# Moving weight-only work of a cross-attention into the feed-forward block in front of it, on one Trainium2 core

## The chip, the cores and the metric

One core of a Trainium2 chip runs the whole program. The metric is the device time of one execution in microseconds (us), as the median of several runs. The engines are named as in the profile: PE (TensorE, matmuls), PEld (its weight loads), DVE (VectorE), ACT (ScalarE), POOL (GpSimd), SP (SyncE, which here only issues DMAs).

## The reference, cut to what matters

Six blocks follow each other on a stream x of 512 rows by 512 columns; each adds its result to x and each starts with a layer norm over the columns. The change touches blocks 3, 4 and 5.

```python
def _layernorm(x, axis=-1, eps=1e-05):
    m = jnp.mean(x, axis=axis, keepdims=True)
    v = jnp.var(x, axis=axis, keepdims=True)
    return (x - m) / jnp.sqrt(v + eps)
...
    x = x + _L0_ffn_ref(_layernorm(x, axis=-1), ...)                 # block 3: w1, depthwise conv, silu, w2, both products quantised
    x = x + _L1_xattn_ref(ctx_1024, _layernorm(x, axis=-1), ...)     # block 4
    x = x + _L1_attn_ref(_layernorm(x, axis=-1), ...)                # block 5
...
    def _L1_xattn_ref(x, latents, Wq, Wkv, Wout, gm, bm, gl, bl):    # x is the context of 8192 rows
        xn = layernorm(x, gm, bm)
        ln = layernorm(latents, gl, bl)                              # a second norm of an already normed tensor
        q = ln @ Wq
        kv_input = jnp.concatenate([xn, ln], axis=-2)
        kv = kv_input @ Wkv
...
        xn = _l2norm(x) * dim ** 0.5 * gamma                         # block 5: unit rows of an already normed tensor
```

## The kernel before

Each engine has one program, written in order by hand; the engines meet through counting semaphores. A float32 product is done as three passes over two parts of each operand (`product`, three matmuls: low by high, high by low, high by high), so each operand is first split into a rounded high part (usually by ACT) and a remainder (by DVE or POOL). The context is handled in 17 chunks of 512 keys; chunk 0 are the latents (the 512 rows of x), chunks 1 to 16 are the context. `cT_raw`, `cT_hi`, `cT_lo` hold a chunk and its halves, two slots in turn.

The work around the change, in the order of PE:

- Block 3. The rows of the normed x are quantised on DVE and ACT (`xq_s`, `xq`), transposed on PE, and a row of factors is spread over the partitions by a matmul with diagonal matrices (`diagonals` on DVE, `spread` on PE, `scale_all` on ACT). Then 16 blocks hb of 128 hidden features: PE multiplies (4 matmuls into one of two banks), DVE scales (`pre_conv`), ACT and DVE do the convolution of three taps, ACT the silu and the absolute value, DVE the running maximum (`col_max`, by `largest`). PE may be two blocks ahead of DVE. Then the maximum is transposed, made into factors, spread again by `diagonals(…, 1)` and `spread(1)`, the hidden rows are scaled and rounded in eight pieces (`hidden_s`, `hidden_q`), and PE does the second product, whose four row blocks come out one after another.
- Block 4, preparation. DVE adds each row block to x and norms it twice (`TWICE`: the order of the two norms of four row blocks). POOL computes the two reciprocal roots of each. PE transposes the rows. `sd` (a reciprocal of the context's scales) is split and transposed. PE multiplies `wkv_raw` by `b_ctx` in matmuls of one column (`bv`). DVE subtracts to get `wq_lo`; it applies gain and offset (`affine_rows`) and splits (`xT_hi`, `xT_lo`). PE computes the queries, then the keys of chunk 0 with `wkv_hi`, `wkv_lo`. For the context the weights are used in another form, `wp_hi`, `wp_lo`: `wkv_raw` times the gain `g_ctx`, minus its column mean (a PE sum with `ones`). Their order on PE is queries, keys, column sum, values. ACT copies chunk 1 into `cT_hi`, POOL subtracts for `cT_lo` after it has set `peak` to its starting value, and only then `project_pe(1, …)` starts: the long loop over the chunks, in which PE also computes similarities of the chunk before for the row maximum.
- Block 5. As in block 4 each row block is added and normed, then squared and summed on ACT, and made a unit row by POOL (power) and DVE (`unit_row`).

The DMAs of all this are issued by SP in a fixed order: the quantised weights (`w_q`) while block 2 ends; `wq_raw`, `wkv_raw` and two context chunks after the last output of block 3's second product.

## Time and profile before

| | |
|---|---|
| time, median of 3 runs | 2752.25 us (2751.64 to 2753.24) |
| the profiled execution: its own time / its span | 2750.85 / 2749.1 us |
| PE, PEld, DVE busy | 2521.2 (92%), 1681.8 (61%), 1842.6 us (67%) |
| ACT, POOL busy | 1106.4 (40%), 566.0 us (21%) |
| block 3 and the preparation of block 4 | about 799 to 963 us of the span |
| the norm of block 5 | about 1981 to 1993 us |

The busy share of an engine is an average over blocks with different limits. The change lies in two stretches, which have to be read by themselves: which engine works there, which waits, and what ends its wait. The time of the profiled execution is 1.75 us above its span, and 1.4 us below the median of the runs.

### The profile page before, as it was taken

The page shows a single profiled execution, that of the slowest core. Times are in us where ns is not written, and L with a number is a line of the kernel's source. Part 1 is how long each engine was busy: PE and PEld are TensorE (multiplying, and loading weights), DVE is VectorE, ACT ScalarE, POOL GpSimd, SP SyncE. Part 2 cuts the span into 40 slices and gives each one's busy share as a digit, 9 for nine tenths or more (in the row PEclk, how much of TensorE's full clock was granted, in tenths as well). Part 3 has the DMA queues.
Part 4 walks back from the last instruction along what each step waited for, and adds up shares of the span by engine and source line. Part 5 has one row for each costly group of instructions (what it writes and reads, how often), then busy time and mean ns, then how long its engine had stood idle before and what let it go on. Part 6 is the DMA issues. An engine that isn't in the chain of part 4 may idle for free.

```text
span 2749.1 us, 33961 instructions
## 1 busy us (share of the span) xinstructions
PE 2521.2 (92%) x11615; PEld 1681.8 (61%) x11618; DVE 1842.6 (67%) x2026; ACT 1106.4 (40%) x1344; POOL 566.0 (21%) x413
## 2 busy tenths in 40 slices
PE   6999988967765799999999999999898799999999
PEld 5778867722222677777765454555477677777775
DVE  5878753189988677778886666666535666666665
ACT  2334422244435322222235555555332455555453
POOL 4555552078850211111110000000100100000000
PEclk9999989999986899999999999999889899999999
DMA  7677745710010233433423332333200366666663
GB/s 281 235 238 261 262 119 161 275 52 16 15 69 12 103 135 135 160 145 132 159 97 109 110 97 66 96 111 96 81 31 31 153 230 224 222 224 219 218 227 134
DMA packets 123659, 394.68 MB, mean 144 GB/s; under 512 B 23664, under 2 KB 39228, under 8 KB 97072
## 3 DMA queue, kind: packets, MB, share of 16 engines
q1 hardware_dynamic: 95584, 326.82, 33.5%
q10 hardware_dynamic: 27984, 66.66, 7.0%
q8 instruction: 56, 0.92, 0.1%
q14 instruction: 35, 0.29, 0.0%
HBM read 304.14 MB, written 89.30 MB: 143 GB/s over the span
## 4 chain that ended last, share of the span: by engine, by line
PE 78%; DVE 10%; DMA 5%; issue 3%; POOL 2%; ACT 1%; ACTq 0%; DVEq 0%; SPq 0%; POOLq 0%
PE ps L2130 18%; PE ps L2131 16%; PE ps L2132 16%; PE ps L2481 10%; PE ps L2491 9%; DVE ps L1632 4%; PE ps L2389 3%; DMA w_halves<-unit_lo 3%; PE ps L2742 1%; DMA wT_lo<-w_halves 1%; DVE drive L1632 1%; PE ps L2283 1%; POOL drive L907 1%; DMA sh_raw<-in_s_parts 1%; DVE ln_st L1478 1%
## 5 line engine op out<-in xcount | busy, mean ns | idle before, releaser
L1877 DVE TENSOR_TENSOR sums<-sums,pT 128x1024 f32<-128x1024 f32 x272 | 319.2, 1221 | 194.0 <-ACT pT L1302 192.9
L1815 DVE SCALAR_TENSOR_TENSOR peak<-ps,rs_all,peak 128x1024 f32<-128x1024 f32 x272 | 335.6, 1278 | 95.0 <-PE ps L2389 94.6
L1302 ACT ACTIVATE pT<-ps,rs_all 128x1024 f32<-128x1024 f32 x272 | 284.9, 1112 | 230.7 <-PE ps L2481 230.4
L2491 PE MATMUL ps<-pT,values 128*64 128x512 f32 x1088 | 256.4, 602 | 0.0
L2235 PE MATMUL ps<-read,ident 128*128 128x512 f32 x256 | 143.7, 673 | 73.8 <-DVE read L1638 37.2
L907 POOL TENSOR_TENSOR drive<-x_conv,bc_all 128x1024 f32<-128x1024 f32 x64 | 150.4, 2372 | 102.0 <-PE ps L2132 102.0
L955 POOL TENSOR_TENSOR cT_lo<-cT_raw,cT_hi 128x512 fp32r<-128x512 f32 x64 | 82.5, 1291 | 347.7 <-ACT cT_hi L1251 347.7
L2491 PEld LDWEIGHTS ps<-pT,values 128*64 128x64 f32 x1088 | 68.8, 136 | 132.9 <-issue 122.3
L2017 DVE TENSOR_TENSOR rgu_lo<-rgu_raw,rgu_hi 128x2048 fp32r<-128x2048 f32 x64 | 143.9, 2288 | 5.2 <-ACT rgu_hi L1390 5.1
L2235 PEld LDWEIGHTS ps<-read,ident 128*128 128x128 f32 x256 | 44.0, 200 | 168.5 <-DVE read L1638 82.7
L1165 ACT ACTIVATE ps<-delta,a_neg 128x512 f32<-128x512 f32 (+1 forms) x128 | 88.4, 692 | 126.7 <-DVE read L1638 113.3
L842 POOL TENSOR_SCALAR ln_ve<-ln_mv 128x1 f32<-128x1 f32 x20 | 7.3, 363 | 619.2 <-DVE ln_mv L1479 619.0
L855 POOL TENSOR_TENSOR ctx_lo<-ctx_raw,ctx_hi 128x512 fp32r<-128x512 f32 x64 | 104.3, 1629 | 126.2 <-DVE ctx_hi L1513 126.2
L1239 ACT ACTIVATE key_hi<-ps 128x512 fp32r<-128x512 f32 x68 | 40.7, 598 | 203.9 <-PE ps L2132 203.9
L2011 DVE TENSOR_TENSOR sh_lo<-sh_raw,sh_hi 128x1536 fp32r<-128x1536 f32 x32 | 56.3, 1758 | 93.4 <-ACT sh_hi L1385 93.4
L1390 ACT ACTIVATE rgu_hi<-rgu_raw 128x2048 fp32r<-128x2048 f32 x64 | 118.8, 1907 | 0.0
L1632 DVE TENSOR_TENSOR_SCAN ps<-ps,drive 128x512 f32<-128x512 f32 x96 | 116.8, 1217 | 2.2 <-POOL drive L907 2.2
L2481 PE MATMUL ps<-q_lo,key_hi 64*128 64x512 f32 x544 | 117.7, 429 | 0.0
L2130 PE MATMUL ps<-cT_hi,wp_lo 128*128 128x512 f32 x256 | 107.8, 421 | 8.9 <-POOL cT_lo L955 8.9
L1244 ACT ACTIVATE values<-ps,rs_all 128x512 f32<-128x512 f32 x68 | 46.8, 688 | 163.5 <-PE ps L2132 163.5
L2130 PE MATMUL ps<-xT_hi,ctxT_lo 128*128 128x512 f32 x256 | 102.2, 399 | 9.2 <-DVE ctxT_lo L1515 9.2
L2481 PE MATMUL ps<-q_hi,key_lo 64*128 64x512 f32 x544 | 107.2, 391 | 0.0
(439 smaller groups left out, 6310.7 us busy)
## 6 DMA issues: line engine op xcount, KB each, us to landing
rgu_raw<-in_r_gate_up SPq DMA_DIRECT2D x64, 1024.0 KB, 4.8
rd_raw<-in_r_down SPq DMA_DIRECT2D x32, 1024.0 KB, 4.8
sh_raw<-in_s_parts SPq DMA_DIRECT2D x32, 768.0 KB, 4.4
key_rows<-key_hi SPq DMA_DIRECT2D x17, 1024.0 KB, 3.9
key_rows<-key_lo SPq DMA_DIRECT2D x17, 1024.0 KB, 5.9
value_rows<-values SPq DMA_DIRECT2D x17, 1024.0 KB, 8.7
ctxT_raw<-in_ctx_T SPq DMA_DIRECT2D x16, 1024.0 KB, 6.7
ctx_raw<-in_ctx SPq DMA_DIRECT2D x16, 1024.0 KB, 8.1
```

The source lines that it names most:

```text
L907: nc.gpsimd.tensor_tensor(drive[:, g % SCAN_AHEAD], x_conv[:, ib].unsqueeze(1).to_broadcast([P, SG, T]), b_all[:, g * SG:(g + 1) * SG], AL ...
L1302: nc.scalar.activation(pT[:, i], ps[:, b:b + 2], ACT.Exp, scale=rs_all[:, bass.ds(c * KT + attend_tile(j, i)[1], 1)]).then_inc(s4_exp.sem, 1)
L1632: nc.vector.tensor_tensor_scan(source if far(g, e) else ps[:, DECAY_BANK + e], ps[:, DECAY_BANK + e], source, 0.0, ALU.mult, ALU.add).then ...
L1815: nc.vector.scalar_tensor_tensor(peak[:, p], ps[:, b:b + 2], rs_all[:, bass.ds(c * KT + kt, 1)], peak[:, p], ALU.mult, ALU.max).then_inc(s ...
L1877: nc.vector.tensor_tensor(sums[:, p], sums[:, p], pT[:, i], ALU.add).then_inc(s4_sum.sem, 1)
L2017: nc.vector.tensor_tensor(rgu_lo[:, j % 2, i], rgu_raw[:, j % 2, i], rgu_hi[:, j % 2, i].bitcast(F32), ALU.subtract).then_inc(rgu_low.sem, 1)
L2130: nc.tensor.matmul(o, l_lo, r_hi, start=start, stop=False)
L2131: nc.tensor.matmul(o, l_hi, r_lo, start=False, stop=False)
L2132: return nc.tensor.matmul(o, l_hi, r_hi, start=False, stop=stop)
L2235: done = nc.tensor.matmul(ps[:, b], ident[:], read[:, g % SCAN_AHEAD, e], start=g == 0 and e == 0, stop=g == SGS - 1 and e == SG - 1)
L2481: done = nc.tensor.matmul(ps[:, b + e], key[rows], query[rows], start=m == 0, stop=m == len(parts) - 1)
L2491: done = nc.tensor.matmul(ps[e * DK:(e + 1) * DK, 6 + p], values[:, s, kt, h * DK:(h + 1) * DK], pT[:, i, e], start=start and kt == 0, sto ...
```

## The change

The change has five parts.

1. The load of `wkv_raw` is issued between the two halves of `w_q`, before block 3; that of `wq_raw` when the first product of block 3 is done; those of the two context chunks half way through the rounding of the hidden rows.
2. What depends on weights alone moves into block 3. On POOL, which did nothing there: the splits `wkv_hi` and `wkv_lo` in quarters, the gain (`w_gained`), and `wq_lo`. On ACT: `wq_hi` after the loop over hb. On PE: the 16 one-column matmuls of `bv` in the blocks 0 to 7, two each, and the column sum (8 matmuls of 128x512) in the blocks 11 to 15, the last four in block 15. On DVE: the copy of `bv` and the centring `w_centred`, two quarters ahead of the wait for the second `scale_all` and two after the rounding.
3. In block 4 PE does queries, transposes of `sd`, keys, values and goes on with chunk 1. Chunk 1 is split while chunk 0 is computed, into the buffers of `xT_hi` and `xT_lo` (as `first_hi`, `first_lo`). The queries start with the first quarter of `xT_lo` instead of the last.
4. The second norm in block 4 becomes a factor in the first: the variance v of the row gives (v(1 + eps) + eps²) to the power -1/2. The unit rows of block 5 likewise, from max(512 v, tiny); the squares on ACT and `unit_row` go.
5. The scaled hidden rows are written in place (`hidden` for `hidden_s`).

```diff
@@ SP
+                if w == 1:
+                    sp.wait_ge(sc_y, IB * SGS)
+                    sp.dma_start(wkv_raw[:], a["L1_xattn_Wkv"]...).then_inc(w4_loaded[1].sem, 16)
                 for c in range(W_CHUNKS):
                     sp.dma_start(w_q[w][:, c], wq_dram[w * W_CHUNKS + c]).then_inc(wq_loaded[w], 16)
-            sp.wait_ge(s3_out, TT)
+            sp.wait_ge(h_product, HB)
             sp.dma_start(wq_raw[:], ...)
-            sp.dma_start(wkv_raw[:], ...)
+            sp.wait_ge(hq_ready, HB // HQ // 2)
             load_chunk(chunks[0], 1)
             load_chunk(chunks[1], 0)
@@ POOL, behind the memset of pre_conv
+            pool.wait_ge(*w4_loaded[1](16))
+            for dt in range(DT):
+                nc.gpsimd.tensor_copy(wkv_hi[:, dt], wkv_raw[:, dt]).then_inc(wkv_high.sem, 1)
+                pool.wait_ge(*wkv_high(dt + 1))
+                nc.gpsimd.tensor_tensor(wkv_lo[:, dt], wkv_raw[:, dt], wkv_hi[:, dt].bitcast(F32), ALU.subtract).then_inc(wkv_low.sem, 1)
+            pool.wait_ge(*wkv_low(DT))
+            pool.wait_ge(*bv_mm(1))
+            for dt in range(DT):
+                nc.gpsimd.tensor_scalar(wkv_raw[:, dt], wkv_raw[:, dt], g_ctx[:, dt:dt + 1], None, ALU.mult).then_inc(w_gained.sem, 1)
+            pool.wait_ge(*w4_hi(1))
+            nc.gpsimd.tensor_tensor(wq_lo[:], wq_raw[:], wq_hi[:].bitcast(F32), ALU.subtract).then_inc(wq_low.sem, 1)
...
-            for n, tt in enumerate((0, 1, 0, 2, 1, 3, 2, 3)):
-                twice_scale(n, tt)
+            for tt in range(TT):
+                twice_scale(tt)
...
+            split_rest(1, 1)
+            pool.wait_ge(*w4_hi(1 + DT))
+            pool.wait_ge(*w4_lo(DT))
+            nc.gpsimd.memset(peak[:], -3.0e38).then_inc(s4_init.sem, 1)
             split_rest(2, 0)
@@ ACT, behind the loop over hb
+            act_e.wait_ge(*w4_loaded[0](16))
+            nc.scalar.activation(wq_hi[:], wq_raw[:], ACT.Copy).then_inc(w4_hi.sem, 1)
             act_e.wait_ge(diag_sum, 2)
...
             for dt in range(DT):
                 act_e.wait_ge(*w_centred(dt + 1))
                 nc.scalar.activation(wp_hi[:, dt], wkv_raw[:, dt], ACT.Copy).then_inc(w4_hi.sem, 1)
-                values_out(0, 0, dt)
-            split_chunk(1, 1, 1, range(KT))
+                split_chunk(1, 1, 1, (dt,))
+                keys_hi(0, 0, dt)
+            for j in range(KT):
+                values_out(0, 0, j)
@@ DVE
+                if hb == HB // 2 + 1:
+                    dve.wait_ge(*bv_mm(1))
+                    nc.vector.tensor_copy(bv[:], ps[:, 5, 0:PAIRS]).then_inc(bv_ready.sem, 1)
...
             row_back(1)
+            weights_centred(0)
+            weights_centred(1)
             dve.wait_ge(scale_ready, 2)
...
             level_out(HB // HQ - 1)
+            weights_centred(2)
+            weights_centred(3)
-            for tt in range(TT + 2):
+            for tt in range(TT + 1):
...
-                if 1 <= tt <= TT:
-                    ln_row(3 * TT + TWICE[0][tt - 1], tt - 1, x_res)
-                    dve.wait_ge(xn_ready, 3 * TT + TWICE[0][tt - 1] + 1)
-                    ln_measure(tt - 1, xn)
-                if tt >= 2:
-                    ln_row(3 * TT + TWICE[1][tt - 2], tt - 2, xn)
+                if tt:
+                    ln_row(3 * TT + tt - 1, tt - 1, x_res)
...
-            weights_lo(1, wq_lo[:], wq_hi[:], wq_raw[:])
@@ PE, loop over hb
+                if hb == 0:
+                    pe.wait_ge(*w4_loaded[1](16))
+                if hb < 2 * PAIRS:
+                    ...   # two one-column matmuls of bv
+                if hb >= HB - 5:
+                    for n in ((hb - (HB - 5),) if hb < HB - 1 else (4, 5, 6, 7)):
+                        half, dt = n % 2, n // 2
+                        if half == 0:
+                            pe.wait_ge(*w_gained(dt + 1))
+                        done = nc.tensor.matmul(ps[:, 6 + half], ones[:], wkv_raw[:, dt, half * D:(half + 1) * D], ...)
+            done.then_inc(wp_sum.sem, 1)
             pe.wait_ge(max_ready, HB)
+            pe.wait_ge(*bv_ready(1))
@@ PE, block 4
-            pe.wait_ge(*a4_low(DT))
-            pe.wait_ge(*w4_lo(1))
+            pe.wait_ge(*wq_low(1))
...
+                    if hp == 0:
+                        pe.wait_ge(*a4_low(dt + 1))
```

What stands in a row on PE in block 3 and after it, before the change (`w_q` is the quantised weight, `ones` as the second name is the operand held still, a name is that of a buffer):

```order
L2271 MATMUL ps<-diag,ones 128x128 x4
L2283 MATMUL ps<-xqT,w_q 128x512 x64
L2287 MATMUL ps<-ident,col_max 128x128 x4
L2271 MATMUL ps<-diag,ones 128x128 x4
L2293 MATMUL ps<-w_q,hidden_q 128x512 x64
L2309 MATMUL ps<-ident,xn 128x128 x16
L2314 MATMUL ps<-ident,sd_parts 68x128 x2
L2319 MATMUL ps<-b_ctx,wkv_raw 128x1 x16
L2130 MATMUL ps<-xT_hi,wq_lo 128x512
```

And the same place after it, from block 7 of the loop on:

```order
L2282 MATMUL ps<-b_ctx,wkv_raw 128x1 x2
L2275 MATMUL ps<-xqT,w_q 128x512 x16
L2291 MATMUL ps<-wkv_raw,ones 128x512
...
L2275 MATMUL ps<-xqT,w_q 128x512 x4
L2291 MATMUL ps<-wkv_raw,ones 128x512 x4
L2297 MATMUL ps<-ident,col_max 128x128 x4
L2263 MATMUL ps<-diag,ones 128x128 x4
L2303 MATMUL ps<-w_q,hidden_q 128x512 x64
L2320 MATMUL ps<-ident,xn 128x128 x16
L2122 MATMUL ps<-xT_hi,wq_lo 128x512
```

The two products of `wkv_raw` now stand inside the loop and in front of the transposes of `col_max`, and nothing stands between the transposes of `xn` and the queries.

POOL from the start of block 3 to the long loop, before:

```order
L933 MEMSET pre_conv 128x1028
L938 TENSOR_SCALAR ln_ve<-ln_mv 128x1
L939 TENSOR_TENSOR ln_rstd<-ln_ve,neg_half 128x1
...
L943 MEMSET scale_rows 128x1024
L947 TENSOR_TENSOR key_lo<-affine,key_hi 128x512 x4
L950 MEMSET peak 128x4096
L955 TENSOR_TENSOR cT_lo<-cT_raw,cT_hi 128x512 x8
```

And after the change:

```order
L934 MEMSET pre_conv 128x1028
L938 CAST wkv_hi<-wkv_raw 128x1024
L940 TENSOR_TENSOR wkv_lo<-wkv_raw,wkv_hi 128x1024
...
L944 TENSOR_SCALAR wkv_raw<-wkv_raw,g_ctx 128x1024 x4
L946 TENSOR_TENSOR wq_lo<-wq_raw,wq_hi 128x2048
L951 TENSOR_SCALAR ln_ve<-ln_mv 128x1
L952 TENSOR_TENSOR ln_rstd<-ln_ve,neg_half 128x1
...
L956 MEMSET scale_rows 128x1024
L960 TENSOR_TENSOR key_lo<-affine,key_hi 128x512 x4
L968 TENSOR_TENSOR xT_lo<-cT_raw,xT_hi 128x512 x4
L973 MEMSET peak 128x4096
L968 TENSOR_TENSOR cT_lo<-cT_raw,cT_hi 128x512 x4
```

Thirteen large instructions came in between the memset of `pre_conv` and the norms (the pair of cast and subtraction stands four times, the pair of norm instructions eight times before and four times after), and the split of chunk 1 went ahead of the memset of `peak`.

## Rows read from the trace of the kernel before

**Rows 1.** The page: shares of the chain that ended last, by engine.

```profile
PE 78%; DVE 10%; DMA 5%; issue 3%; POOL 2%; ACT 1%; ACTq 0%; DVEq 0%; SPq 0%; POOLq 0%
```

**Rows 2.** Windows, us: length, PE, PEld, DVE, ACT, POOL busy, granted clock, DMA.

```profile
827.00:855.00 28.00, 19.99 (x43) 4.51 (x41) 27.60 (x44) 20.53 (x32) 0.00 (x0) 0.50 0.00 1
```

**Rows 3.** Timeline of PE: start us, length us, line, operands, count, idle before.

```profile
903.57 6.83 PE L2319 MATMUL ps<-b_ctx,wkv_raw 128*128 128x1 f32 x32
...
910.82 0.79 PE L2130 MATMUL ps<-xT_hi,wq_lo 128*128 128x512 f32 x1 [0.42 <-DVE xT_lo L1780]
...
925.62 0.47 PE L2130 MATMUL ps<-key_hi,wkv_lo 128*128 128x512 f32 x1 [1.50 <-DVE q_lo L1769]
...
936.62 7.03 PE L2372 MATMUL ps<-wkv_raw,ones 128*128 128x512 f32 x16
...
963.42 0.79 PE L2130 MATMUL ps<-cT_hi,wp_lo 128*128 128x512 f32 x1 [8.88 <-POOL cT_lo L955]
```

**Rows 4.** Timeline of DVE, from the last row blocks of block 3 on.

```profile
886.90 0.75 DVE L1737 SCALAR_TENSOR_TENSOR x_res<-ps,t_back,x_res 128x512 f32<-128x512 f32 x1 [2.17 <-PE ps L2293]
...
900.96 1.14 DVE L1484 TENSOR_SCALAR xn<-xn,ln_mv,ln_rstd 128x512 f32<-128x512 f32 x1 [0.76 <-POOL ln_rstd L939]
...
903.18 2.29 DVE L1765 TENSOR_TENSOR wq_lo<-wq_raw,wq_hi 128x2048 fp32r<-128x2048 f32 x1
905.39 2.96 DVE L1760 TENSOR_SCALAR affine<-ps,g_lat,b_lat 128x512 f32<-128x512 f32 x4
...
943.69 2.36 DVE L1799 SCALAR_TENSOR_TENSOR wkv_raw<-ps,wkv_raw 128x1024 f32<-128x1024 f32 x2 [5.55 <-PE ps L2372]
```

**Rows 5.** Timeline of DVE, first and last row of block 3's norm, then of block 5's.

```profile
800.70 0.69 DVE L1657 TENSOR_TENSOR x_res<-ps,x_res 128x512 f32<-128x512 f32 x1 [3.74 <-PE ps L2132]
...
809.01 1.15 DVE L1484 TENSOR_SCALAR xn<-x_res,ln_mv,ln_rstd 128x512 f32<-128x512 f32 x1 [0.77 <-POOL ln_rstd L843]
...
1980.73 0.69 DVE L1916 TENSOR_TENSOR x_res<-ps,x_res 128x512 f32<-128x512 f32 x1 [3.48 <-PE ps L2132]
...
1991.98 1.14 DVE L1911 TENSOR_SCALAR xn<-xn,sum_sq 128x512 f32<-128x512 f32 x1 [0.81 <-POOL sum_sq L982]
```

**Rows 6.** Timeline of POOL, at two places.

```profile
808.92 0.95 POOL L933 MEMSET pre_conv<- 128x1028 f32 x1
...
898.02 0.42 POOL L938 TENSOR_SCALAR ln_ve<-ln_mv 128x1 f32<-128x1 f32 x1 [0.30 <-DVE ln_mv L1479]
```

**Rows 7.** Timeline of DVE, beside the second row of POOL.

```profile
897.85 0.52 DVE L1484 TENSOR_SCALAR xn<-xn,ln_mv,ln_rstd 128x512 f32<-128x512 f32 x1
898.28 0.54 DVE L1484 TENSOR_SCALAR xn<-x_res,ln_mv,ln_rstd 128x512 f32<-128x512 f32 x1
```

**Rows 8.** One line of DVE in block 1: duration in ns, min/median/max.

```profile
L1515 DVE TENSOR_TENSOR ctxT_lo<-ctxT_raw,ctxT_hi x64: 674/680/1687, 27.0 to 378.0; 128x512 fp32r<-128x512 f32 x64
```

**Rows 9.** POOL by form: count, busy us, mean ns, idle before.

```profile
L907 POOL TENSOR_TENSOR drive<-x_conv,bc_all 128x1024 f32<-128x1024 f32 x64 | 150.4, 2372 | 102.0 <-PE ps L2132 102.0
...
L888 POOL CAST xc_hi<-x_conv 128x512 fp32r<-128x512 f32 x2 | 1.2, 610 | 2.7 <-ACT x_conv L1102 2.7
```

**Rows 10.** DVE in block 3: timeline, and by form the running maximum.

```profile
813.13 1.67 DVE L1682 TENSOR_SCALAR xq_s<-xn,t_scale 128x512 f32<-128x512 f32 x4
...
814.98 0.87 DVE L1675 TENSOR_SCALAR diag<-ident,t_back 128x128 f32<-128x128 f32 x4
...
866.32 0.87 DVE L1675 TENSOR_SCALAR diag<-ident,t_scale 128x128 f32<-128x128 f32 x4
...
L1694 DVE TENSOR_TENSOR col_max<-col_max,h_abs 128x512 f32<-128x512 f32 x15 | 10.3, 685 | 0.7 <-ACT h_abs L1204 0.7
```

**Rows 11.** DMA: issue on SP (start, length), and one load's issue to landing, us.

```profile
794.39 3.76 SPq L678 DMA_DIRECT2D w_q<-w_quantised  x8
...
wkv_raw<-in_L_xattn_Wkv SPq DMA_DIRECT2D x1, 2048.0 KB, 10.2
```

**Rows 12.** Timeline of ACT, one of four.

```profile
952.54 1.05 ACT L1258 ACTIVATE wp_hi<-wkv_raw 128x1024 fp32r<-128x1024 f32 x1
```

More of the change, by code:

```diff
@@ L132 @@
 TINY = 1e-24
-SQUARED = (1, 2, 4, 6)
-UNIT_ROWS = [5 * TT + n for n in (3, 5, 7, 8)]
-TWICE = ((0, 1, 3, 5), (2, 4, 6, 7))
 class Signal:
@@ L333, in build @@
         wq_raw = over("wq_raw", [P, DT, D])
-        over.at += 8192
         wq_hi = over("wq_hi", [P, DT, D], F32R)
-        wq_lo = over("wq_lo", [P, DT, D], F32R)
         over = Map(nc, at, s4.at)
@@ L362, in build @@
         q_lo = s4("q_lo", [P, PAIRS, T], F32R)
+        first_hi, first_lo = (half[:].rearrange("p t n -> p (t n)").rearrange("p (k t n) -> p k t n", k=KT, n=P) for half in (xT_hi, xT_lo))
         at = s4.at
@@ L539, in build @@
             "act", "w4_hi", "a4_hi", "q_hi", "k_hi", "v", "cT_split", "exp", "o_hi", "sd_out", "shift_ready", "inv_out", "o_saved0")
-        (w4_lo, a4_aff, a4_low, q_lo_ready, k_lo, s4_peak, s4_sum, o_lo, s4_x, sd_split, bv_ready, w_gained, w_centred,
+        (w4_lo, a4_aff, a4_low, q_lo_ready, k_lo, s4_peak, s4_sum, o_lo, s4_x, sd_split, bv_ready, w_centred,
          peak_neg, shift_split, o_inv, o_norm, o_saved1) = again(
-            "dve", "w4_lo", "aff", "aff_lo", "q_lo", "k_lo", "peak", "sum", "o_lo", "x", "sd_split", "bv", "w_gained", "w_centred",
+            "dve", "w4_lo", "aff", "aff_lo", "q_lo", "k_lo", "peak", "sum", "o_lo", "x", "sd_split", "bv", "w_centred",
             "peak_neg", "shift_split", "o_inv", "o_norm", "o_saved1")
-        s4_init, a4_lo, cT_rest, rs_step = again("pool", "init", "a4_lo", "cT_rest", "rs_step")
+        s4_init, a4_lo, cT_rest, w_gained, wkv_high, wkv_low, wq_low = again(
+            "pool", "init", "a4_lo", "cT_rest", "w_gained", "wkv_hi", "wkv_lo", "wq_lo")
         def retire(engine, *counts):
@@ L947, in _ @@
                 nc.gpsimd.tensor_tensor(lat_lo[:, dt], affine[:, dt], lat_hi[:, dt].bitcast(F32), ALU.subtract).then_inc(a4_lo.sem, 1)
-            pool.wait_ge(*w4_hi(2 + DT))
-            pool.wait_ge(*w4_lo(2 + DT))
-            nc.gpsimd.memset(peak[:], -3.0e38).then_inc(s4_init.sem, 1)
             def split_rest(c, s):
@@ L1221, in queries_hi @@
                 nc.scalar.activation(q_hi[:, hp], ps[:, 2 + hp % 2], ACT.Copy, scale=SIM_SCALE).then_inc(q_hi_ready.sem, 1)
-            act_e.wait_ge(*w4_loaded[0](16))
-            nc.scalar.activation(wq_hi[:], wq_raw[:], ACT.Copy).then_inc(w4_hi.sem, 1)
+            affine_hi(0, xT_hi)
+            affine_hi(1, lat_hi)
+            for hp in range(PAIRS):
+                queries_hi(hp)
             act_e.wait_ge(*sd_T(1))
@@ L1227, in _ @@
                                  ACT.Copy).then_inc(sd_out.sem, 1)
-            affine_hi(0, xT_hi)
-            act_e.wait_ge(*w4_loaded[1](16))
-            nc.scalar.activation(wkv_hi[:], wkv_raw[:], ACT.Copy).then_inc(w4_hi.sem, 1)
-            affine_hi(1, lat_hi)
-            for hp in range(PAIRS):
-                queries_hi(hp)
             def keys_hi(c, s, hp, turn=0):
@@ L1249, in split_chunk @@
                         act_e.wait_ge(*cT_loaded[s](turn * 16))
-                        act_e.wait_ge(*v_mm((c - 1) * KT))
-                    nc.scalar.activation(cT_hi[:, s, j], cT_raw[:, s, j], ACT.Copy).then_inc(cT_split.sem, 1)
-            for hp in range(PAIRS):
-                keys_hi(0, 0, hp)
+                        if not (isinstance(c, int) and c == 1):
+                            act_e.wait_ge(*v_mm((c - 1) * KT))
+                    to = first_hi[:, j] if isinstance(c, int) and c == 1 else cT_hi[:, s, j]
+                    nc.scalar.activation(to, cT_raw[:, s, j], ACT.Copy).then_inc(cT_split.sem, 1)
             act_e.wait_ge(*q_mm(PAIRS))
@@ L1333, in _ @@
             qkv_hi(1)
-            for tt in range(TT):
-                act_e.wait_ge(xn_ready, 5 * TT + SQUARED[tt])
-                nc.scalar.activation(squares[:, tt], xn[:, tt], ACT.Square, accum_out=sum_sq[:, tt:tt + 1]).then_inc(x5_sq.sem, 1)
             act_e.wait_ge(*g5_ready(1))
@@ L2366, in _ @@
                 project_key(0, hp, (wkv_hi, wkv_lo), lambda dt: [half[:, dt] for half in lat])
-            pe.wait_ge(*w_gained(DT))
             pe.wait_ge(*sd_out(1))
-            pe.wait_ge(*bv_ready(1))
-            for half in range(2):
-                for dt in range(DT):
-                    done = nc.tensor.matmul(ps[:, half], ones[:], wkv_raw[:, dt, half * D:(half + 1) * D], start=dt == 0, stop=dt == DT - 1)
-            done.then_inc(wp_sum.sem, 1)
             for j in range(KT):
```

176 lines of the change are left out of this document (80 added, 96 removed).

## The prediction

> **What bounds the kernel now.** The chain that ended last is PE for 78% [rows 1], so time is lost where PE waits for something else. I read the windows of the stretch from 799 to 963 us, then the timelines of PE, DVE, POOL and ACT there. Block 3's loop is not PE's: in its 28 us DVE is busy for 27.60 and PE for 19.99, at a granted clock of 0.50, the lower of its two levels, 1.2 GHz [rows 2]. POOL does nothing. 43 matmuls, four to a block, make 10.6 blocks: one lasts 2.65 us and holds 1.9 of PE. Block 4's preparation is a series of waits. DVE norms four row blocks twice, from 886.90 to 902.10, and subtracts `wq_lo` before it touches the transposed rows at 905.39 [rows 4]; the queries start at 910.82, the keys at 925.62 after 1.50 idle, the column sum takes 7.03, and chunk 1 starts at 963.42 after 8.88 idle, because POOL split it last [rows 3]. From there PE has no such gaps, so what the preparation saves comes off the end.
>
> **What the change takes away.**
>
> Second norm. Its twin without a second norm is in block 3: from the first add at 800.70 to the end of the last row at 809.01 + 1.15 = 810.16, 9.5 us [rows 5]. Block 4 adds with the slower form (0.75 for 0.69 [rows 4, 5]), so 9.7 for 15.2: 5.5 less. The two late centring steps are 2.36 together and DVE has 2.17 idle before the first add [rows 4]: 0.2 back. Net 5.3.
>
> `wq_lo` between norm and affine: 905.39 - 902.10 = 3.3, of which `wq_lo` is 2.3 and small steps of `sd` the rest [rows 4]; the last transposes stay. 2.3 to 2.9, I take 2.6. POOL must have `wq_lo` by about 900; by what follows it is ready near 880.
>
> Queries by quarters: the four affines end at 908.35, PE starts at 910.82 [rows 3, 4], so a subtraction is 0.62 and three are no longer waited for: 1.8.
>
> The one-column matmuls (6.83) ended at 910.40, before `xT_lo` [rows 3]; taking them out gains nothing by itself. The 1.50 before the keys goes (all waits for `wkv_lo` and `q_lo` are met or moved), the transposes of `sd` come in: 0.9 (0 to 1.5).
>
> The column sum: keys last 925.62 to 936.62, 11.0. Sum and values end at 963.42 - 8.88 = 954.54, which is 17.9; less 11.0 for the values and 0.4 of overlapping tail, the sum is 6.5 of the path.
>
> The gap of 8.88 goes if chunk 1 is split during keys and values, 22 us. ACT has four rounds of three casts there, none longer than 1.05 [rows 12], at most 12.6; POOL four subtractions of 128x512 and a memset, under 10; so 8.9 whole. After an idle stretch PE ran the 48 matmuls of the queries in 910.82 to 924.12, 13.3, while the same number for the keys took 11.0 [rows 3]: a restart costs up to 2.3. Chunk 1 has such a restart now and none then: 1.3 (0 to 2.3).
>
> Block 5: from 1980.73 to 1993.12 is 12.4 [rows 5], its twin 9.5: 2.9. ACT's squares cover nothing else.
>
> Together 5.3 + 2.6 + 1.8 + 0.9 + 6.5 + 8.9 + 1.3 + 2.9 = 30.2.
>
> **What it costs.** All of it lies in block 3, where DVE sets the pace.
>
> First, POOL and DVE get in each other's way. The memset of POOL at 808.92 ends at 809.87; DVE's last `xn` began at 809.01 and took 1.15 [rows 5, 6], against 0.52 for the same instruction with POOL out of the way [rows 7]: it ended 0.3 after the memset. The same shows at 900.96 and 1991.98, where 1.14 stands for about 0.5 [rows 4, 5]. A DVE subtraction with two SBUF operands, 0.67 at best, took up to 1.69 in block 1 [rows 8]. So a DVE instruction of these kinds waits for the whole POOL instruction. The Trainium skill (GPSIMD Engine Reference, Key points) says that POOL shares its SBUF interfaces with DVE, against DVE's two-port modes and instructions with two SBUF inputs; the trace agrees, and adds that the wait runs to the instruction's end.
>
> Who wins when both queue? At 897.85 and 898.28 DVE ran two such instructions back to back, and a POOL instruction that came at 898.02 was over at 898.44, before the second DVE one was [rows 6, 7]: POOL slips in between. So I expect turns.
>
> Now price it. A cast of 128x512 is 0.61 on POOL, so 128x1024 about 1.1; a subtraction of 128x1024 like L907, 2.35 [rows 9]. Four pairs are 14 us, 15 with their own waits. `wkv_raw` is issued near 796.3, after four of the eight `w_q` loads of 794.39 to 798.15; with 10.2 to landing [rows 11] it is there before POOL is free at 809.9. So POOL works from 810 to 825 and more, and DVE makes its four roundings (0.4 each) from 813.13 and four diagonals (0.2 each) from 814.98 [rows 10], eight instructions of the kind that waits, on the path to the first block. In turns, the first waits 0.75 for the subtraction in progress, and three casts and two subtractions (8.0) go in ahead of the last diagonal: 8.75, of which PE's transposes hide a little. I take 8.0. The low end is 0.3, if POOL yields to a queue of DVE; the high end 12, if all that POOL has left goes first.
>
> Second, in the loop only `col_max` (0.69, two SBUF operands [rows 10]) can be hit. POOL's four gains begin after the `bv` matmuls, in blocks 7 to 10; each hit waits half an instruction: 1.2 (0 to 3). The copy of `bv` adds 0.2.
>
> Third, `wq_lo` on POOL is one instruction of 128x2048, twice L907: 4.7 [rows 9]. It can start once ACT has made `wq_hi` (1.9, twice the 1.05 [rows 12]) behind the last block, near 865, and the second set of diagonals, 866.32 [rows 10], waits for its end. That is on the path to `scale_all`: 3.0 (0 to 4.7). The centring steps behind it fit the wait for `scale_all`. The skill's page (GPSIMD Engine Reference, Elementwise — side-by-side cycle accounting) has 4497 ns for such an addition on POOL against 2293 on DVE; the trace's DVE row, 2.29, agrees, and by the page this term would be 0.2 less.
>
> Fourth, PE. Two `bv` matmuls per block are 6.83 / 8 = 0.85: 2.75 for 2.65, eight times 0.1, inside the block by which PE is ahead. A column-sum matmul is 0.9 at full clock, 1.8 at the clock of the loop: at worst PE falls 1.0 behind in four blocks and has 7 us of sums before the transposes of `col_max`, 2.8 late; at full clock nothing. POOL's delays of DVE leave PE room. I take 0.3.
>
> Fifth, `sd`'s two port-bound steps on DVE now meet POOL's `lat_lo`, and the low half of the first query stands behind them: 0.4 (0 to 1.5).
>
> SP: the wait for `sc_y` holds back only the second half of `w_q`, needed 60 us later; the context chunks come early enough.
>
> Together 8.0 + 1.2 + 0.2 + 3.0 + 0.3 + 0.4 = 13.1. The net is 30.2 - 13.1 = 17.1. The profiled execution's own time is 2750.85, so 2733.7; the median of the runs is 1.4 above it: **2735.1**, 2735 rounded.
>
> **The rivals.**
>
> *Turns at the port (my forecast)*, 0.5: 2728 to 2741.
>
> *The port costs little.* POOL yields to a queue, or `wkv_raw` lands late and the pairs run inside the loop, where most DVE instructions read PSUM. For it: scan and convolution steps in block 2 kept their time beside POOL. Against: the rows above. Losses of 1 to 5 give 2722 to 2727. 0.22.
>
> *The port costs more.* The tiny `t_max` steps wait too, and the gains are as slow as subtractions, with the column sum at half clock: up to 12 + 3 + 4.7 + 2.8 + 1.5, gains at their low ends, 27.7: 2741 to 2749. 0.2, since several would have to meet.
>
> *No change that can be measured.* Chunk 1's early start is given back, the long loop being held by something other than PE: only what comes ahead of it counts, 30.2 - 13.1 less 10 to 15. Against: no gap of PE behind 963.42. 2748 to 2756. 0.05.
>
> *Slower.* One mechanism: DVE's waiting instructions come behind everything that POOL has queued, through the loop too, and `col_max` holds every block while a gain or a pair stands: 15 + 4 x 2.35 + 4.7 = 29 us of POOL in front of DVE. It decides from 30.2 on; PE's 2.8 would tip it: 2754 to 2758. The interleaving at 898.02 speaks against. 0.03.
>
> **How the numbers follow.** The likeliest case gives 2735. 2723 to 2744 leaves out the cheapest part of the second case (under 0.1) and the dear half of the third with the last two (about 0.15); forecast alone: 2728 to 2741. About 0.2% (5.5 us) is what a measurement of this kernel can tell from no change. Faster by more than that, below 2746.7: 0.92; within it 0.06; slower 0.02.
>
> **What would show it.** Rightly: POOL busy with pairs from 810; a `xq_s` or `diag` group of several us where 1.67 and 0.87 stood; the first product of block 3 some 8 us later; the second `diag` group 3 to 4 us long; from the first add of block 4 to its last row 9.7; chunk 1's first matmul right behind the values, 26 to 27 us nearer to the first add than the 76.5 of before; block 5's norm 9.5. It is wrong if `wkv_raw` lands after 812 (pairs late), if POOL's casts at 128x1024 are far from 1.1, if PE waits for `w_gained` or `wq_low`, or if the first groups of chunk 1 wait for `peak`.

## The result, and the profile after

The changed kernel takes 2732.97 us (median of 4 runs, 2729.31 to 2734.68), the kernel before 2752.17 in the same comparison (2751.64 to 2753.24): a ratio of 0.9928, 95% interval 0.9911 to 0.9945. It is 19.2 us faster; 17.1 were forecast. The profiled execution's own time is 2734.27, its span 2732.5.

The page of the changed kernel, shares of the chain that ended last:

```profile
PE 79%; DVE 12%; DMA 4%; issue 3%; POOL 1%; ACT 1%; DVEq 0%; ACTq 0%; SPq 0%; POOLq 0%
```

This answers to [rows 1]: a little more DVE, a little less POOL and DMA. It doesn't say where. The timelines do. First POOL from the start of block 3 to its end:

```profile
810.42 0.95 POOL L934 MEMSET pre_conv<- 128x1028 f32 x1
811.32 1.22 POOL L938 CAST wkv_hi<-wkv_raw 128x1024 fp32r<-128x1024 f32 x1
812.62 2.35 POOL L940 TENSOR_TENSOR wkv_lo<-wkv_raw,wkv_hi 128x1024 fp32r<-128x1024 f32 x1
814.91 1.04 POOL L938 CAST wkv_hi<-wkv_raw 128x1024 fp32r<-128x1024 f32 x1
816.03 2.34 POOL L940 TENSOR_TENSOR wkv_lo<-wkv_raw,wkv_hi 128x1024 fp32r<-128x1024 f32 x1
...
823.28 2.40 POOL L940 TENSOR_TENSOR wkv_lo<-wkv_raw,wkv_hi 128x1024 fp32r<-128x1024 f32 x1
845.09 11.35 POOL L944 TENSOR_SCALAR wkv_raw<-wkv_raw,g_ctx 128x1024 f32<-128x1024 f32 x4 [19.41 <-PE ps L2282]
875.83 4.49 POOL L946 TENSOR_TENSOR wq_lo<-wq_raw,wq_hi 128x2048 fp32r<-128x2048 f32 x1 [19.39 <-ACT wq_hi L1217]
```

And DVE in the same stretch, then at the second product, block 4 and block 5:

```profile
811.69 2.29 DVE L1686 TENSOR_REDUCE t_max<-xn 128x4 f32<-128x2048 f32 x1
814.01 0.98 DVE L1672 TENSOR_SCALAR t_max<-t_max 128x4 f32<-128x4 f32 x1
...
815.24 0.73 DVE L1674 TENSOR_SCALAR t_scale<-t_scale 128x4 f32<-128x4 f32 x1
816.01 7.47 DVE L1689 TENSOR_SCALAR xq_s<-xn,t_scale 128x512 f32<-128x512 f32 x4
823.40 2.31 DVE L1677 TENSOR_SCALAR t_back<-t_max,w_mean 128x4 f32<-128x4 f32 x1
825.74 0.87 DVE L1682 TENSOR_SCALAR diag<-ident,t_back 128x128 f32<-128x128 f32 x4
...
851.61 0.81 DVE L1701 TENSOR_TENSOR col_max<-col_max,h_abs 128x512 f32<-128x512 f32 x1
...
854.39 0.85 DVE L1701 TENSOR_TENSOR col_max<-col_max,h_abs 128x512 f32<-128x512 f32 x1
...
876.60 3.74 DVE L1672 TENSOR_SCALAR t_max<-t_max 128x4 f32<-128x4 f32 x1
...
901.33 0.74 DVE L1758 SCALAR_TENSOR_TENSOR x_res<-ps,t_back,x_res 128x512 f32<-128x512 f32 x1
...
909.81 1.14 DVE L1491 TENSOR_SCALAR xn<-x_res,ln_mv,ln_rstd 128x512 f32<-128x512 f32 x1 [0.71 <-POOL ln_rstd L952]
...
911.59 2.96 DVE L1770 TENSOR_SCALAR affine<-ps,g_lat,b_lat 128x512 f32<-128x512 f32 x4 [0.58 <-PE ps L2320]
...
1966.18 0.69 DVE L1910 TENSOR_TENSOR x_res<-ps,x_res 128x512 f32<-128x512 f32 x1 [4.50 <-PE ps L2124]
...
1974.47 1.14 DVE L1491 TENSOR_SCALAR xn<-x_res,ln_mv,ln_rstd 128x512 f32<-128x512 f32 x1 [0.76 <-POOL ln_rstd L996]
```

While POOL makes its four pairs, from 811.32 to 823.28 + 2.40 = 825.68, every scaling or clipping (TENSOR_SCALAR) of DVE from SBUF to SBUF is longer than it needs: the four roundings `xq_s` take 7.47 where 1.67 stood [rows 10]. The reduction at 811.69 isn't: it takes 2.29, as in the kernel before, beside a cast and a subtraction of POOL. The four diagonals come after 825.68 and take their old 0.87. The one `t_max` step at 876.60, four elements wide, ends at 880.34, just when `wq_lo` on POOL does (875.83 + 4.49 = 880.32). Yet the four running maxima under the four gains take 0.68, 0.68, 0.81 and 0.85, 0.30 us more than their own times in all. The last gain, for the last of them:

```profile
853.60 2.84 POOL L944 TENSOR_SCALAR wkv_raw<-wkv_raw,g_ctx 128x1024 f32<-128x1024 f32 x1
```

A maximum that begins 0.80 us after its gain ends as if it had started at 0.97 (854.39 + 0.85 - 0.68 - 853.60 = 0.96 from these rounded rows); the one at 851.61, 0.84 after its own gain, gives 0.97 too. Those that begin 1.02 and 1.23 us after theirs are not held at all.

PE, where it answers to [rows 3]:

```profile
828.97 1.47 PE L2275 MATMUL ps<-xqT,w_q 128*128 128x512 bf16 x3 [0.22 <-issue]
...
915.30 0.77 PE L2122 MATMUL ps<-xT_hi,wq_lo 128*128 128x512 f32 x1 [3.18 <-DVE xT_lo L1790]
...
939.69 0.39 PE L2122 MATMUL ps<-wkv_hi,key_lo 128*128 128x512 f32 x1
```

The queries follow the first affine by 3.71 (5.43 before). Keys start at 928.68, values at 939.69, chunk 1 at 950.57 with no idle time ahead of it. The spans part stage by stage like this (us; each row is a difference of two starts on the timelines):

| stretch | before | after | difference |
|---|---|---|---|
| start of the program to block 3's first add | 800.70 | 802.20 | +1.50 |
| to block 3's first product | 17.83 | 26.77 | +8.94 |
| to the end of the last `col_max` | 45.23 | 45.69 | +0.46 |
| to the second diagonals | 2.56 | 6.13 | +3.57 |
| to block 4's first add | 20.58 | 20.54 | -0.04 |
| to the end of the last `xn` of block 4 | 15.20 | 9.62 | -5.58 |
| to the first affine | 3.29 | 0.64 | -2.65 |
| to the queries | 5.43 | 3.71 | -1.72 |
| to the keys | 14.80 | 13.38 | -1.42 |
| to the values | 17.47 | 11.01 | -6.46 |
| to chunk 1 | 20.33 | 10.88 | -9.45 |
| to block 5's first add | 1017.31 | 1015.61 | -1.70 |
| to the end of block 5's last `xn` | 12.39 | 9.43 | -2.96 |
| to the end | 755.98 | 756.89 | +0.91 |

The sum is -16.6, the difference of the spans. The first and last rows lie where nothing was changed: over the profiles taken here the first runs from 800.4 to 811.3 and the last from 749.8 to 756.9. Without them the change is worth -19.0, close to the 19.2 of the medians. Single rows move from profile to profile as well: the loop, 45.69 here, is 46.04 to 46.52 in the four other profiles whose edit leaves it as it is (the changed kernel again and experiments 2, 5 and 6), and the stretch from chunk 1 to block 5, 1015.61 here, is 1013.96 in the second profile of the changed kernel.

### The profile page after: what moved, and what is told of

The parts are those of the page before. It is cut to its first block, busy times and chain, and to the rows that moved or that the text cites. A ratio compares the mean times of both kernels' runs of the same rounds, so it can differ in the third digit from the quotient of the medians.

```text
span 2732.5 us, 33932 instructions
## 1 busy us (share of the span) xinstructions
PE 2516.2 (92%) x11614; PEld 1682.0 (62%) x11618; DVE 1843.3 (67%) x2003; ACT 1100.8 (40%) x1335; POOL 592.3 (22%) x410
## 4 chain that ended last, share of the span: by engine, by line
PE 79%; DVE 12%; DMA 4%; issue 3%; POOL 1%; ACT 1%; DVEq 0%; ACTq 0%; SPq 0%; POOLq 0%
PE ps L2122 18%; PE ps L2123 17%; PE ps L2124 17%; PE ps L2481 10%; PE ps L2491 9%; DVE ps L1639 4%; PE ps L2388 3%; DMA w_halves<-unit_lo 2%; DVE drive L1639 1%; PE ps L2742 1%; DMA sh_raw<-in_s_parts 1%; DVE ln_st L1485 1%; DMA x_res<-in_x 1%; POOL drive L908 1%; DVE read L1645 0%
## 5 line engine op out<-in xcount | busy, mean ns | idle before, releaser
L995 POOL TENSOR_SCALAR ln_ve<-ln_mv 128x1 f32<-128x1 f32 x4 | 1.5, 379 | 538.5 <-DVE ln_mv L1486 538.5
L2481 PE MATMUL ps<-q_hi,key_hi 64*128 64x512 f32 x544 | 106.9, 390 | 0.0
```

Source lines behind the costliest of these rows:

```text
L2481: done = nc.tensor.matmul(ps[:, b + e], key[rows], query[rows], start=m == 0, stop=m == len(parts) - 1)
```

## The experiments

All are edits of the changed kernel, except the fourth. Their ratios are to runs of the kernel before on the same chip: 2752.99 us for 1 to 4, 2750.82 for 5 to 8, 2748.58 (one run) for 9 and 10.

**1. Pairs behind the diagonals.** POOL's four pairs wait until DVE has made its diagonals, and so run inside the product loop.

```diff
             pool.wait_ge(*w4_loaded[1](16))
+            pool.wait_ge(diag_ready, 1)
```

> The changed kernel, except that POOL waits for the first set of diagonals of block 3 before it begins the casts and subtractions of wkv. Theory (DVE takes turns with whole POOL instructions at a shared port): the four roundings take 1.7 again instead of 7.5 and t_back 0.2 instead of 2.3, the first product of block 3 comes 17.8 us after the block's first add instead of 26.8, and the pairs in the loop hit only col_max, for some 0.5 to 1.5 us in all: 8 us less, a median of 2724 to 2726. Rival (the late start of block 3 comes from the 2 MB load of wkv_raw ahead of the second half of w_q, or from PE's wait for it): the first product stays at 26 to 27 us and the median at 2732 to 2734.

Measured: 2726.49 us (2726.22 to 2726.69), ratio 0.9906 [0.9892, 0.992]. From block 3's first add to the first product 17.27 us, 9.5 less than in the changed kernel; the loop 48.09, 2.4 more. The median is 0.5 above the range that was expected; the loss in the loop is more than the 0.5 to 1.5 expected. Two timeline rows of DVE in the loop, where 0.42 and 0.68 stand without POOL:

```profile
828.31 2.22 DVE L1704 COPY col_max<-h_abs 128x512 f32<-128x512 f32 x1
...
832.49 1.92 DVE L1702 TENSOR_TENSOR col_max<-col_max,h_abs 128x512 f32<-128x512 f32 x1
```

The same pairs meet two instructions there instead of seven, since what else DVE does in the loop keeps its time. The load of `wkv_raw` is where it was, so the rival that blames the load is out: the 8.9 us are DVE's waits for these pairs. It is also the second rival's place (the pairs inside the loop), reached by an edit.

**2. `wq_lo` behind the second row factors.** POOL's one instruction of 128x2048 waits until the last of the hidden rows is rounded.

```diff
             pool.wait_ge(*w4_hi(1))
+            pool.wait_ge(hq_ready, HB // HQ)
             nc.gpsimd.tensor_tensor(wq_lo[:], ...)
```

> The changed kernel, except that POOL subtracts for wq_lo only when the last of the hidden rows is rounded. Theory (the second t_max step waits for the whole 4.5 us instruction of POOL): that step takes 0.2 instead of 3.7, the second scale_all comes 3.5 us earlier; the subtraction then runs beside the last centring and the first adds, which do not use the port; POOL's first reciprocal root is at most 0.7 late. Median 2729 to 2731. Rival (POOL's late subtraction pushes the norms back by as much, since POOL works in order): the first rows of the norm are 3 us late and the median stays at 2732 to 2734.

Measured: 2731.53 us (2726.11 to 2735.13), ratio 0.9921 [0.9906, 0.9936], not told apart from the changed kernel by the time alone. In the trace the tiny step is short again, and `wq_lo` ends at 906.08, after block 4's first add at 903.75:

```profile
882.42 0.17 DVE L1673 TENSOR_SCALAR t_max<-t_max 128x4 f32<-128x4 f32 x1
```

```profile
901.55 4.53 POOL L947 TENSOR_TENSOR wq_lo<-wq_raw,wq_hi 128x2048 fp32r<-128x2048 f32 x1 [39.32 <-DVE hidden_q L1744]
```

The stretch to the second diagonals is 2.56 again, the norm's to the first affine 10.41 for 10.26: 3.4 us less in these two stretches, as the theory has it. The median, 2731.53, is 0.5 above the expected range. The run reached block 3 5.1 later than the changed kernel's profile.

**3. Both moves.**

> The changed kernel with both moves: the pairs wait for the first diagonals, wq_lo for the last rounding. If the two waits at the port are what block 3 pays, the two gains add up: 11 to 12 us less than the changed kernel, 2721 to 2723. Rival (with the first taken away POOL runs late in the loop, the gains come late and PE waits for them before the column sum, so the transposes of col_max come late): 2725 or more.

Measured: 2723.34 us (2718.07 to 2723.93), ratio 0.9888 [0.9873, 0.9903]. First product after 17.31, loop 48.07, second diagonals after 2.56: 10.7 less than the changed kernel up to there, 9.6 in the medians, 0.3 above what was expected. In the profile the loop's 2.4 is already counted; another 0.3 comes back in the norm of block 4 (9.94 for 9.62) and 0.6 between the queries and chunk 1, and what made the latter isn't shown.

**4. The norms alone**: part 4 of the change, applied to the kernel before.

> The kernel before with the single norms of blocks 4 and 5 alone; nothing else is moved. If norms simply add up, block 4 gives 5.5 and block 5 gives 2.9: 8.4 less, 2743.8. Theory: in block 4 the one-column matmuls of bv (6.8 us on PE, behind the load of wkv_raw that lands about 900 us) were covered by the longer norm and come out in front of the queries, so block 4 gives only about 4 and the total is 2745 to 2746.

Measured: 2745.93 us (2741.24 to 2752.2), ratio 0.9979 [0.9968, 0.999]. Block 4's first add to first affine: 12.93 for 18.49, -5.6. Block 5: 9.45 for 12.39, -2.9. But what follows shows what is late next. PE's timeline:

```profile
900.30 6.99 PE L2299 MATMUL ps<-b_ctx,wkv_raw 128*128 128x1 f32 x32 [1.98 <-DMA wkv_raw<-in_L_xattn_Wkv]
```

With the norm shorter, the load of `wkv_raw`, which the kernel before issues late, holds the one-column matmuls, and these the queries: 7.21 from affine to queries instead of 5.43. The forecast's 5.3 for the second norm holds only with the load moved, as the whole change does.

**5. Chunk 1 split late again.** ACT's roundings of the chunk go back behind the values, POOL's subtraction with them.

```diff
@@ ACT
-                split_chunk(1, 1, 1, (dt,))
...
                 values_out(0, 0, j)
+            split_chunk(1, 1, 1, range(KT))
@@ POOL
-            split_rest(1, 1)
             pool.wait_ge(*w4_hi(1 + DT))
             pool.wait_ge(*w4_lo(DT))
             nc.gpsimd.memset(peak[:], -3.0e38)...
+            split_rest(1, 1)
```

> The changed kernel, with ScalarE's roundings of chunk 1's projection weight back behind the values of chunk 0 and GpSimd's subtraction back behind them too. My theory: the gap before chunk 1 was made by this split alone, so nearly all of it comes back: the stretch from the first product of the values to the first product of chunk 1, 10.88 us in the changed kernel and 20.33 before it, is 19.5 to 20.5 again, and the whole is about 9 to 11 us above the changed kernel (near 2743). Rival: other work (VectorE's values, the restart of TensorE at its lower clock) sets a good part of the gap; then the stretch grows by less than 6 us. Both stages before it should stay as in the changed kernel within 0.5 us.

Measured: 2743.04 us (2738.24 to 2747.18), ratio 0.9973 [0.9959, 0.9987]. The total came as expected; the stretch did not. From the values to chunk 1 it is 17.43, 6.55 more than in the changed kernel but 2.9 less than before. PE's row, then POOL's two:

```profile
965.65 0.79 PE L2122 MATMUL ps<-xT_hi,wp_lo 128*128 128x512 f32 x1 [6.39 <-POOL xT_lo L968]
```

```profile
948.91 3.53 POOL L972 MEMSET peak<- 128x4096 f32 x1 [16.95 <-DVE wp_lo L1775]
960.68 4.92 POOL L968 TENSOR_TENSOR xT_lo<-cT_raw,xT_hi 128x512 fp32r<-128x512 f32 x4 [8.24 <-ACT xT_hi L1263]
```

The memset of `peak` waits for DVE's last `wp_lo`. That was done by 948.91 here, because the centring had gone into block 3. POOL's rows of the kernel before at the same place:

```profile
954.98 3.51 POOL L950 MEMSET peak<- 128x4096 f32 x1 [36.83 <-DVE wp_lo L1765]
958.45 2.48 POOL L955 TENSOR_TENSOR cT_lo<-cT_raw,cT_hi 128x512 fp32r<-128x512 f32 x2
```

There DVE's last `wp_lo` ends at 954.85, and POOL subtracts only after the memset, at 958.45, though ACT's first rounding had ended at 955.88: 2.57 late, for 0.08 here (960.60 to 960.68). So of the 9.45 us, 6.55 belong to the early split, and the other 2.9 almost whole to the memset, which the move of the column sum and the centring had already freed. This is read from the two traces; no run moves the memset alone. My expectation gave all of it to the split. The restart shows in the windows after chunk 1's first product, of this kernel and then of the changed one:

```profile
965.65:975.00 9.35, 9.35 (x35) 7.10 (x36) 4.13 (x4) 1.81 (x3) 1.29 (x1) 0.81 0.66 240
```

```profile
950.57:960.00 9.43, 9.43 (x45) 6.82 (x44) 4.65 (x5) 2.50 (x4) 1.29 (x1) 1.00 0.84 323
```

After the idle stretch the granted clock is 0.81 over 9.35 us, without it 1.00: 0.19 x 9.35 = 1.8 us. From chunk 1 to block 5 it is 1017.34 here, 1017.31 in the kernel before, and 1013.96 to 1015.72 in the profiles without a gap: 1.6 to 3.4 less, with the 1.8 inside a scatter as large as itself.

**6. The pairs in halves.** Casts and subtractions of 128x512, sixteen instructions for eight.

```diff
             for dt in range(DT):
-                nc.gpsimd.tensor_copy(wkv_hi[:, dt], wkv_raw[:, dt])...
+                for half in range(2):
+                    cols = slice(half * D, (half + 1) * D)
+                    done = nc.gpsimd.tensor_copy(wkv_hi[:, dt, cols], wkv_raw[:, dt, cols])
...
```

> The changed kernel, with GpSimd's casts and subtractions of the key and value weights in pieces of 128x512 instead of 128x1024: sixteen instructions for eight, the same elements. Theory of turns (VectorE waits at each instruction of its own until the one that GpSimd has begun is done): each wait is half as long and the number of VectorE's instructions that meet one grows, so the four scalings of the chunk, 7.47 us as a group in the changed kernel and 6.7 unhindered, take 4.5 to 7.5 us, the first small instruction of the row factors waits about 0.6 to 1.2 us less, and the stretch from block 3's first addition to the first product, 26.8 us, becomes 24.5 to 26.8. Rival, that the two engines share bandwidth in proportion to what they move: the stretch stays at 26.8 within 0.3, since the elements are the same. In all 0 to 2 us below the changed kernel.

The 6.7 us in this expectation is an error of mine: unhindered, the four scalings take 1.67 [rows 10]. Measured: 2731.31 us (2716.99 to 2736.03), ratio 0.9914 [0.9888, 0.9941]. DVE's timeline:

```profile
823.06 1.25 DVE L1680 TENSOR_SCALAR t_max<-t_max 128x4 f32<-128x4 f32 x1
...
824.90 4.33 DVE L1697 TENSOR_SCALAR xq_s<-xn,t_scale 128x512 f32<-128x512 f32 x4
829.15 0.57 DVE L1685 TENSOR_SCALAR t_back<-t_max,w_mean 128x4 f32<-128x4 f32 x1
829.76 3.69 DVE L1690 TENSOR_SCALAR diag<-ident,t_back 128x128 f32<-128x128 f32 x4
```

The four scalings cost 2.66 over their 1.67 instead of 5.80 (4.33 in all, a little below the expected 4.5 to 7.5), and the four diagonals now meet POOL too, 3.69 for 0.87. To the first product 24.55 for 26.77, 2.2 less with the same elements moved: the stretch follows the length of POOL's instructions, as turns say and shared bandwidth does not. The first step waited 0.3 longer instead of less, against my expectation; what it meets hangs on when it comes.

**7. Both moves and halves.**

> Both GpSimd moves (the pairs behind the diagonals, the low part of the query weight behind the second row factors), and the pairs in halves. Against the kernel with both moves alone, in which two of VectorE's running maxima in the product loop lasted about 2.2 and 1.9 us instead of 0.69, turns say that these are at most 1.2 us each and that the whole is 1 to 2 us shorter (2721 to 2722.5); bandwidth says no difference within 0.5 us in the trace.

Measured: 2722.27 us (2719.7 to 2729.4), ratio 0.9901 [0.9885, 0.9918]. The three running maxima that meet the pairs:

```profile
829.00 0.53 DVE L1713 COPY col_max<-h_abs 128x512 f32<-128x512 f32 x1
...
831.49 0.82 DVE L1711 TENSOR_TENSOR col_max<-col_max,h_abs 128x512 f32<-128x512 f32 x1
...
834.28 0.94 DVE L1711 TENSOR_TENSOR col_max<-col_max,h_abs 128x512 f32<-128x512 f32 x1
```

They cost 0.5 over their own times where whole pairs cost 3.0. From the first add to the end of the last maximum it is 64.13 for 65.38, so 1.25 of the 2.5 reached the path; the rest is lost at the start of the product, which begins 0.5 later and takes 0.7 longer to its first result on DVE. The medians differ by 1.1, but their intervals overlap, so only the trace tells this kernel from the one with both moves. The two are the fastest versions timed here.

**8. The changed kernel again**, beside 5 to 7.

> The changed kernel as it is, for the comparison on this chip: 2729 to 2735, ratio 0.991 to 0.9945.

Measured: 2732.32 us (2730.96 to 2736.59), ratio 0.9939 [0.9924, 0.9953]; the stretches of the table from block 3's first product to block 5's first add agree with the first profile within 0.6 each, but for the long one after chunk 1 (1.65 less).

**9. Gains as a product of two tensors.** The gains on POOL hardly touched the maxima. Is it their form?

```diff
-                nc.gpsimd.tensor_scalar(wkv_raw[:, dt], wkv_raw[:, dt], g_ctx[:, dt:dt + 1], None, ALU.mult)...
+                nc.gpsimd.tensor_tensor(wkv_raw[:, dt], wkv_raw[:, dt], g_ctx[:, dt:dt + 1].to_broadcast([P, 2 * D]), ALU.mult)...
```

> The changed kernel, with GpSimd's four gains of the key and value weight (128x1024, one operand and a factor for each partition, 2.84 us each, during which VectorE's running maxima lasted 0.68 to 0.85 us instead of 0.68) written as a product of two tensors, the second the factor spread over the row. If it is the operation with two tensors read from memory that takes turns with VectorE, the maxima under the gains wait up to 2.3 us each and the loop (first product to the last maximum's end, 45.7 us in the changed kernel) becomes 47.5 to 50. If the blocking hangs on the stretch of the program and not on the form, the loop stays within 0.5 us.

Measured once: 2731.21 us. POOL, then DVE:

```profile
843.76 8.34 POOL L944 TENSOR_TENSOR wkv_raw<-wkv_raw,g_ctx 128x1024 f32<-128x1024 f32 x4 [19.92 <-PE ps L2282]
```

```profile
845.03 1.17 DVE L1701 TENSOR_TENSOR col_max<-col_max,h_abs 128x512 f32<-128x512 f32 x1
...
848.16 2.18 DVE L1701 TENSOR_TENSOR col_max<-col_max,h_abs 128x512 f32<-128x512 f32 x1
```

The same values in 8.34 us instead of 11.35, and yet the maxima wait 2.0 us instead of 0.3, and the loop is 47.95 for 45.69 and 46.24 in the two profiles of the changed kernel. The maximum at 845.03 begins 1.27 us after its product of two tensors and waits 0.5; the one that began 1.23 after a gain in the changed kernel didn't wait. It is the form.

**10. Casts as a multiplication by one for each partition**, the converse.

```diff
-                nc.gpsimd.tensor_copy(wkv_hi[:, dt], wkv_raw[:, dt])...
+                nc.gpsimd.tensor_scalar(wkv_hi[:, dt], wkv_raw[:, dt], ones[:, 0:1], None, ALU.mult)...
```

> The changed kernel, with GpSimd's four casts of the key and value weight (128x1024, 1.04 to 1.23 us each) written as a multiplication by a factor of one for each partition, the form of the gains. If that form leaves VectorE alone, VectorE's scalings and diagonals wait only behind the four subtractions (2.35 us each), the casts themselves take about 2.8 us each, and the stretch from block 3's first addition to the first product, 26.8 us, is 24 to 27 with waits that all end with a subtraction. If the form holds VectorE up just as a cast does, the first small instruction of the row factors waits longer than its 3.74 us and the stretch is 28 to 33 us.

Measured once: 2723.55 us; the stretch to the first product 24.24 for 26.77. POOL and DVE:

```profile
811.20 3.02 POOL L938 TENSOR_SCALAR wkv_hi<-wkv_raw,ones 128x1024 fp32r<-128x1024 f32 x1
814.31 2.34 POOL L940 TENSOR_TENSOR wkv_lo<-wkv_raw,wkv_hi 128x1024 fp32r<-128x1024 f32 x1
816.63 3.07 POOL L938 TENSOR_SCALAR wkv_hi<-wkv_raw,ones 128x1024 fp32r<-128x1024 f32 x1
...
822.16 2.84 POOL L938 TENSOR_SCALAR wkv_hi<-wkv_raw,ones 128x1024 fp32r<-128x1024 f32 x1
```

```profile
813.85 0.40 DVE L1672 TENSOR_SCALAR t_max<-t_max 128x4 f32<-128x4 f32 x1
...
814.49 2.18 DVE L1674 TENSOR_SCALAR t_scale<-t_scale 128x4 f32<-128x4 f32 x1
816.71 1.32 DVE L1689 TENSOR_SCALAR xq_s<-xn,t_scale 128x512 f32<-128x512 f32 x1
...
818.73 1.25 DVE L1689 TENSOR_SCALAR xq_s<-xn,t_scale 128x512 f32<-128x512 f32 x1
...
822.24 1.11 DVE L1682 TENSOR_SCALAR diag<-ident,t_back 128x128 f32<-128x128 f32 x1
```

The step at 814.49 ends at 816.67, with the subtraction (816.65), as both sides of the expectation have it. Beside the casts in the new form neither side holds. The first scaling begins 0.08 us after the cast of 816.63 and takes 1.32 for its own 0.48, as if it had started 0.92 into the cast; the first diagonal takes 1.11 for its own 0.27, as if it had started 0.91 into the cast of 822.16. The two scalings and the three diagonals behind them, 1.1 to 1.7 us into their casts, take their own times (the second scaling 0.48). The fourth scaling, begun 2.10 us in, takes 1.25 and ends 0.28 behind the cast, as a scaling ends behind a subtraction that held it in the changed kernel (818.65 behind 818.37). The tiny step at 813.85 takes 0.40 for 0.17 and ends at 814.25, with its cast (814.22). So this form holds DVE through about its first 0.9 us and again near its end, and lets it through between. The maxima of the changed kernel came to the gains 0.80 to 1.23 us in, on the edge of the open part; that is why they lost so little.

POOL needs 21.5 us for what took 14.4, and DVE loses 2.5 less, since five of its instructions slip through the open part of two casts. Of the 8.8 us between this one run and the median of the changed kernel, the trace explains these 2.5; of the rest 3.5 to 7.1 lie behind block 5's last row (749.82, for 753.32 and 756.89 in the two profiles of the changed kernel), where nothing was changed.

## Why the prediction was right, point by point

**The bound.** Block 3 was DVE's and everything behind it PE's. Right: what the preparation saved came off the end.

**Second norm**, 5.3 forecast, 5.58 measured; the 0.2 that the two late centring steps were to give back isn't there (-0.04). Experiment 4 gives 5.6 for the edit alone.

**`wq_lo` off DVE**, 2.6 and 2.65. **Queries by quarters**, 1.8 and 1.72. **Idle time before the keys**, 0.9 less 0.4 for `sd`, and 1.42. The bound of 1.5 was nearer than the middle: `sd` behind the queries costs next to nothing. **Column sum**, 6.5 and 6.46. **Block 5**, 2.9 and 2.96.

**Gap before chunk 1**, 8.9, and 9.45 with the tail. The amount was right, its cause only in part: experiment 5 shows 6.55 from the early split, and the two traces put the other 2.9 to the memset, which was freed by the moves of the column sum and the centring. **Restart**, 1.3, and 1.70; experiment 5 gives it as 1.8 by the clock. The second profile of the changed kernel has 3.35 in the same stretch, so the row alone couldn't tell.

**Turns between POOL and DVE**, 8.0 and 8.94. The mechanism is the forecast one (experiments 1, 6, 10). The sum had eight waiting instructions, the four roundings and the four diagonals, and left out the steps of four elements. It let three casts and two subtractions go in after the first wait, without saying why not all six instructions that POOL had left; the trace has all six. The trace has seven: the tiny `t_max` and `t_scale` steps 0.81 and 0.56, the roundings 5.80, `t_back` 2.09 over their own 0.17, 0.17, 1.67 and 0.22; the diagonals come too late to meet anything. That is 9.3, of which 0.3 were hidden. The tiny steps belonged to the rival in which the port costs more; they waited here, and the rest of that rival didn't come.

**`wq_lo` on POOL**, 3.0 and 3.57. The place was wrong: not the diagonals but the `t_max` step ahead of them waited, and so longer. The duration, 4.7 by L907 [rows 9], was 4.49; the Trainium skill (GPSIMD Engine Reference, Elementwise — side-by-side cycle accounting) has 4497 ns, and the trace agrees with it.

**Gains and PE's sums in the loop**, 1.2 + 0.2 + 0.3, and 0.46 for all three. This is the term that was most off. The step that failed is "each hit waits half an instruction": it priced the gains, 2.84 us each, like casts and subtractions, to whose end DVE waits. The maxima waited 0.00, 0.00, 0.13 and 0.17: this form holds DVE only through its first 0.97 us, and the maxima came 0.80 to 1.23 us in. Experiment 9 shows that it is the form, experiment 10 that it is the moment too: a gain whose start fell together with a maximum's would have cost some 0.9 us, by an estimate from these rows. That the maxima came when they did is luck. The loop as a whole is less sure than this wait: over the profiles it grew by 0.5 to 1.3.

By the table the gains are 31.9 for the forecast 30.2 and the costs 13.0 for 13.1 (`sd` is in the gains there), 19.0 net for the 17.1 forecast. That the costs agree is luck in part: the two waits on POOL were forecast 1.5 too low and the loop 1.2 too high. What is left of the difference lies in the gains, above all the idle time before the keys (0.9 with `sd`), the gap (0.5) and the restart (0.4).

**The rivals.** That the port costs little holds for the loop only, and experiment 1 shows what it would have been worth in whole: 7.1 us in the profile, 6.5 between the two medians (6.1 by the ratios). No change and slower are out.
